# Four residual convolution blocks on one core: the halo transfers of the circular convolution move from SP's queue to Pool's

## The reference, cut to what matters

```python
x = x + _L0_conv_ref(_gn(x), L0_conv_W, L0_conv_b)      # 4x4 lattice of 3x3 convolutions with relu
x = x + _L1_conv_ref(_gn(x), L1_conv_weight)            # circular 3x3 convolution (written with FFTs)
x = x + _L2_conv_ref(_gn(x), ...)                       # spline convolution: silu and 8 basis functions
x = x + _L3_conv_ref(_gn(x), L3_conv_combinator, ...)   # plain 3x3 convolution
```

## Time and profile before

| | us |
|---|---|
| median of 3 runs | 1353.57 (1351.46 to 1354.47) |
| the profiled execution | 1358.18 |
| its span in the trace | 1356.4 |

### The profile page before, as it was taken

How to read it: one execution, slowest core, us unless ns; L and a number is a source line. 1 busy time by engine, 2 the same in 40 slices (tenths; PEclk the granted TensorE clock), 3 DMA queues, 4 the chain that set the end, 5 groups by cost and what they waited for, 6 DMA issues and landing times.

```text
span 1356.4 us, 14842 instructions
## 1 busy us (share of the span) xinstructions
PE 1188.7 (88%) x5088; PEld 882.0 (65%) x5088; DVE 770.5 (57%) x946; ACT 700.4 (52%) x740; POOL 505.8 (37%) x810
## 2 busy tenths in 40 slices
PE   1289999999999999999999999999965568888884
PEld 0265677766666677766666677777744446766663
DVE  5489972465565422364646512566434498988732
ACT  2377864453444434444435434433323698988721
POOL 5654655443512043423133147764632231000002
PEclk9999999999999999999999999999977878888888
DMA  9599989999999686999999788886632144466564
GB/s 90 141 265 245 273 262 277 217 216 189 198 191 224 172 206 189 244 192 199 187 191 229 173 251 238 235 228 176 141 62 47 26 74 69 78 98 97 95 98 62
DMA packets 107215, 232.12 MB, mean 171 GB/s; under 512 B 41332, under 2 KB 55236, under 8 KB 98948
## 3 DMA queue, kind: packets, MB, share of 16 engines
q1 hardware_dynamic: 73888, 131.34, 48.4%
q0 software_dynamic: 32704, 99.57, 27.3%
q10 hardware_dynamic: 548, 0.27, 0.2%
HBM read 122.05 MB, written 85.75 MB: 153 GB/s over the span
## 4 chain that ended last, share of the span: by engine, by line
PE 63%; DVE 11%; SPq 9%; DMA 5%; ACT 5%; issue 4%; POOL 3%; DVEq 0%; ACTq 0%; POOLq 0%
PE PB L1646 51%; PE PB L1617 10%; SPq L750 7%; DVE F L1400 2%; DMA S<-lattice 2%; DVE F L1388 2%; DVE F L1474 1%; ACT F L1088 1%; SPq L736 1%; SPq L778 1%; ACT F L1198 1%; POOL taps L834 1%; PE PB L1608 1%; DMA S<-in_x 1%; DMA lattice<-S 1%
## 5 line engine op out<-in xcount | busy, mean ns | idle before, releaser
L1646 PE MATMUL PB<-F,WA 128*96 128x512 f32 (+1 forms) x3792 | 916.9, 403 | 35.7 <-DVE F L1400 25.3
L1646 PEld LDWEIGHTS PB<-F,WA 128*96 128x96 f32 (+1 forms) x3792 | 661.4, 175 | 281.9 <-issue 39.1
L1099 ACT ACTIVATE S<-PB,BIAS 96x512 f32<-96x512 f32 (+1 forms) x320 | 211.7, 682 | 314.7 <-PE PB L1646 314.2
L1088 ACT ACTIVATE F<-S 128x2116 fp32r<-128x2116 f32 (+4 forms) x160 | 261.2, 1633 | 199.8 <-DMA S<-lattice 164.0
L994 POOL DMA_DIRECT2D lattice<-S x240 | 130.7, 554 | 515.1 <-ACT S L1099 496.6
L1388 DVE TENSOR_TENSOR F<-S,F 128x1089 fp32r<-128x1089 f32 (+2 forms) x80 | 121.4, 1518 | 214.8 <-ACT F L1088 214.3
L1617 PE MATMUL PB<-F,WA 128*128 128x512 f32 x576 | 159.4, 440 | 36.2 <-DVE F L1474 36.2
L1400 DVE CAST F<-F 64x528 fp32r<-64x528 f32 (+4 forms) x304 | 186.3, 662 | 3.5
L1390 DVE TENSOR_TENSOR F<-S,F 128x1058 fp32r<-128x1058 f32 x64 | 80.7, 1262 | 184.1 <-ACT F L1088 183.3
L1617 PEld LDWEIGHTS PB<-F,WA 128*128 128x128 f32 x576 | 122.2, 214 | 68.6 <-issue 37.7
L809 POOL TENSOR_TENSOR RS<-VE,NHALF 128x1 f32<-128x1 f32 (+1 forms) x25 | 19.7, 787 | 170.7 <-DVE VE L1313 170.6
(11 more groups left out here) (124 smaller groups left out, 778.9 us busy)
## 6 DMA issues: line engine op xcount, KB each, us to landing
lattice<-S POOLq DMA_DIRECT2D x48, 817.5 KB, 7.0
S<-lattice SPq DMA_DIRECT2D x448, 66.1 KB, 5.5
lattice<-S POOLq DMA_DIRECT2D x96, 272.5 KB, 4.5
S<-lattice SPq DMA_DIRECT2D x160, 136.1 KB, 2.7
S<-lattice SPq DMA_DIRECT2D x72, 272.5 KB, 5.3
S<-lattice SPq DMA_DIRECT2D x160, 70.1 KB, 2.7
S<-lattice SPq DMA_DIRECT2D x80, 136.2 KB, 5.4
S<-lattice SPq DMA_DIRECT2D x160, 66.0 KB, 3.0
```

The source lines that it names most:

```text
L1088: act.activation(piece_view(s, h, 0), raw_view(s, h), ACT.Copy).then_inc(hi_ready, 1)
L1099: act.activation(wide(to[:, at:at + TS])[:, :, 0:RX], pixels(RING_BANK[n % SLOTS_O][0:cell.rows, :]), ACT.Relu, bias=BIAS[0:cell.rows, k:k ...
L1646: last = nc.tensor.matmul(bank, WA[0:rows, first:first + cell.rows], wide(FZ[0:rows, i % SLOTS_F, base:base + TS])[:, :, 0:RX], start=j == ...
```

## The change

`l1_halos` leaves SP's list and enters Pool's. The 8 transfers per image, their sources and destinations, the semaphore that they raise (`l1_halo`), and the wait in front of them (`l1_lo`) stay as they are; only the issuing engine and the place in its list differ. On Pool, `l1_halos(b-2)` stands in step b between `norm_event(0, b-1)` and `norm_event(1, b-5)`. `l1_halos(6)` follows `norm_event(0, 7)`, and `l1_halos(7)` comes after the wait for the end of cell 15 and two memsets, ahead of `norm_event(1, 4)`. SP's loop over the steps holds nothing but input loads and the loads of taps.

```diff
@@ -728,13 +728,6 @@
-            def l1_halos(j):
-
-                z = j % SLOTS_1
-                sp.wait_ge(l1_lo, j + 1)
-                for dst, src in image_halos(F1[:, z, :, 0:TS], F1[:, z, :, TS:2 * TS], True):
-                    sp.dma_start(dst, src).then_inc(l1_halo[z], 16)
-
@@ -751,10 +744,6 @@
-                if k == NC - 1 and b >= 4:
-                    l1_halos(b - 4)
-            for j in range(4, B):
-                l1_halos(j)
@@ -925,6 +914,13 @@
+
+            def l1_halos(j):
+
+                z = j % SLOTS_1
+                pool.wait_ge(l1_lo, j + 1)
+                for dst, src in image_halos(F1[:, z, :, 0:TS], F1[:, z, :, TS:2 * TS], True):
+                    pool.dma_start(dst, src).then_inc(l1_halo[z], 16)
@@ -995,13 +991,17 @@
                 else:
                     if b >= 1:
                         norm_event(0, b - 1)
+                    if b >= 2:
+                        l1_halos(b - 2)
                     if b >= 5:
                         norm_event(1, b - 5)
             norm_event(0, B - 1)
+            l1_halos(B - 2)
             norm_event(1, 3)
             pool.wait_ge(out_done, TOTCH)
             pool.memset(L3S[0][:, 1].bitcast(F32), 0.0).then_inc(l3_clear, 1)
             pool.memset(FR[:, 2, 1].bitcast(F32), 0.0)
+            l1_halos(B - 1)
             norm_event(1, 4)
```

## The result

| | before | after |
|---|---|---|
| median | 1352.5 us (4 runs, 1347.6 to 1354.5) | 1332.7 us (4 runs, 1330.6 to 1339.0) |
| the profiled execution, and its span | 1358.2, 1356.4 | 1339.0, 1336.0 |

The ratio is estimated at 0.9869 (that of the two medians is 0.9854), with a 95% interval of 0.9832 to 0.9906: 13 to 23 us faster. Forecast were 1335.5 and a range of 1329 to 1347.5. The two spans, 20.4 us apart, divide at marks that both traces have; the stage runs from the end of cell step 3 (PE's first `group_means` behind it) to ACT's start of `l1_rows(6)`.

What follows compares the result with a forecast made beforehand. Bound at the lattice's end: a ring through SP's queue, no compute engine. `l1_rows(6)` was to start at 1048.4 instead of 1066.48, 18.1 us earlier, taking the median from 1353.57 to 1335.5 us; range 1329 to 1347.5.

Steps and rivals of the forecast that it cites:

- The ring through SP's queue: Last cell: SP's loads wait behind halo groups, which wait for DVE, which waits for those loads; 17.1 us a group.
- the change of engine: Halo group's path, first issue to use: 6.3 us from Pool, the same as from SP; the gain is the order alone.
- Price of an issue: Pool's halo transfers in the last cell: 0.54 us each on average, between 0.50 and 0.91.
- Landing: Halo transfers issued by Pool: 2.5 us until landed, taken between 2.3 from SP and 2.6 from Pool.
- First halo: Halo group 0, from its start at about 993.8 until PE runs `l1_step(0)`: 7.2 us, where SP's took 8.6.
- The turn of two images: Lattice end after the change: update, halo group, one `l1_step` and a cell step, some 22.5 us per two images.
- Pool's own list holds the last norm: Before `l1_rows(6)`: `norm_event(0, 6)` is held by Pool's list and no longer by DVE, 0.9 us given back.
- rivals 1 and 2: Pool is the bound at 0.91 us an issue: 1343.2 us, 20%; issues held by DVE, mean 1.53 us: 1361, 8%.
- Nothing behind it is lost: From `l1_rows(6)` on: the 18.1 us are carried to the end of the program unshortened.
- the prediction's own sign: Last stage, from `l1_rows(6)` to the end, keeps its old length of 290 us.
- rival 4: PE keeps its clock: `l1_step(0)` and `(2)` at 3.1 us, 3.8 us more won, 1331.7 us; chance 8%.

Runs made afterwards that it cites:

- the one with the slowest Pool: The changed kernel with three chained Pool memsets of 198 columns behind each halo issue; 1363.9 us against 1356.2 for the kernel beside it.
- the divided version: Against the changed kernel, SP issues one side of each image's halos behind its loads, Pool the other side; 1327.9 us, ratio 0.9823.

## Why the prediction was right, and where its steps were off

The direction, the size and the mechanism held: 18.1 us forecast; the medians differ by 19.8 and the spans by 20.4. That the sum came so near is in part luck: the stage won 2.6 us more than forecast and blocks 2 and 3 took 3.3 less, against 5.1 more at the end. By its steps:

- *The ring through SP's queue* was read rightly and is shown: the halos behind the loads on SP give the whole gain. The prediction held the change of engine to be worth nothing on a group's path. It is worth 2.1 us of the stage in the pair measured side by side (the three runs with all halos on SP behind the loads had 53.6 to 54.7, those with all on Pool and nothing added to Pool or DVE 51.5 to 52.5). Groups 2 and 4 too take 6.4 to 6.5 us on SP and 5.4 to 5.5 on Pool from first issue to use. The loss is in group 0. There Pool issues `spread_kan` transfers beside SP's halos (from 987.26, SP from 987.30), and behind its own (996.61 after 992.56); that this is the cause was not tested.
- *Price of an issue*, put at 0.54: 0.504. *Landing*, put at 2.5 us: 2.1. *First halo*, put at 7.2 us: 5.5. These three terms make the schedule's stage, 54.9 us (993.5 to 1048.4), 2.6 longer than the 52.3 measured. The turn of two images, put at 22.5 us, was 21.3 (group 2 from 1015.02, group 4 from 1036.31).
- *Pool's own list holds the last norm*: right, 0.8 us against the 0.9 forecast. The schedules of rivals 1 and 2 held when their prices were brought about, in one run each.
- *Nothing behind it is lost*: wrong by a term that the sum did not have. Pool's DRAIN took 5.1 us more. The row stood in the trace of before (2.27 us), and nothing in it told that it would grow. In the profiled execution it was partly hidden by 3.3 us that blocks 2 and 3 took less; the prediction's own sign, 290 us from `l1_rows(6)` to the end, came out at 291.8. That stretch was 282.1 to 283.2 us in the four kernels with all halos on SP, 279.4 to 282.9 in nine with all or half of them on Pool, and 288.0 in the one with the slowest Pool. Whether some 2 us of it belong to the change, or only to how its last matmuls meet the granted clock (the last twelve took 5.46 us before and 4.60 after), is open.
- *The clock* (rival 4) did not come true: `l1_step(0)` took 5.46 us and `(2)` 4.79. The granted clock of 994 to 1044 us rose from 0.73 to 0.84; PE was busy 28.93 us of these 50 before and 36.74 after. It is the divided version in which `l1_step(2)` ran at 3.10.

```profile
994.00:1044.00 50.00, 28.93 (x98) 22.53 (x98) 16.06 (x42) 14.74 (x22) 9.10 (x15) 0.73 0.30 57
```

```profile
994.00:1044.00 50.00, 36.74 (x137) 29.35 (x138) 24.81 (x73) 18.76 (x30) 35.71 (x69) 0.84 0.25 36
```

(Before and after: length, busy us of PE, weight loads, DVE, ACT and Pool with their instructions, then PEclk, DMA share, GB/s.)

## What to carry to other kernels

Before a transfer is moved to another engine, try to put it behind what it blocks in its own list: here that alone gave the whole gain, and about a third as much again came from dividing a group between two queues. Look in the chain of waits for a turn that comes back to the same queue; its length is the sum of issues, landing and work on the way, and a queue that only waits in the ring costs too. Count the end of the program as well: here 64 transfers that Pool issued came back as 5.1 us in its last DRAIN.

## What the hardware showed that was not expected

- Pool's DRAIN at the end of the program grew with the halo transfers that Pool had issued: 2.27, 4.81 and 7.42 us for 0, 32 and 64, though all of them had landed some 260 us earlier.
- Pool issued these transfers from SBUF to SBUF faster than SP did, 0.50 against 0.63 us from start to start, with a median landing of 2.1 us against 2.3.
- DVE copies of 64x1024 fp32 took 0.71 us each and held a Pool issue by up to 0.33 us; additions of the same size took about 1.2 us each (4.97 for four) and held none.
